# Second weight product of two MLPs with tokens on the output partitions, added to x straight from PSUM

## The reference, cut to what matters

```python
# layer 0
x_in = x
h = film(rmsnorm(x, norm2_w), cond, film2_w, film2_b)
h = gelu(h @ mlp_w1 + mlp_b1) @ mlp_w2 + mlp_b2        # 256 -> 1024 -> 256
x = x_in + h
# layer 1
h = rmsnorm(x, g2) * (1 + scale2) + shift2
a, gate = split(h @ w_fc + b_fc)                        # 256 -> 2048
x = x + (a * silu(gate)) @ w_fo + b_fo                  # 1024 -> 256
```

## Time and profile before

| | us |
|---|---|
| median of 3 runs | 2149.85 (2148.05 to 2149.91) |
| the profiled execution | 2150.09 |
| its span on the core | 2148.3 |
| TensorE busy | 2049.8 (95%) |
| VectorE busy | 1314.9 (61%) |
| ScalarE busy | 987.4 (46%) |
| GpSimd busy | 405.0 (19%) |
| mean granted TensorE clock | 0.993 of full |

### The profile page before, as it was taken

One profiled execution on the slowest core, in us unless ns is written; L12 is line 12 of the kernel. 1 busy time (PEld: TensorE's weight loads), 2 busy tenths in 40 slices (PEclk: granted clock), 3 DMA queues, 4 the chain that ended last, 5 costly groups with the idle time before them and its releaser, 6 DMA issues.

```text
span 2148.3 us, 44435 instructions
## 1 busy us (share of the span) xinstructions
PE 2049.8 (95%) x15652; PEld 1670.8 (78%) x15652; DVE 1314.9 (61%) x2537; ACT 987.4 (46%) x1581; POOL 405.0 (19%) x381
## 2 busy tenths in 40 slices
PE   7999999999999999999999999998999999998998
PEld 6887887778777888877777777776888777787887
DVE  5856565767766565654444555456666677775664
ACT  3444555444444333334444444445444555454443
POOL 3632112223221010101111111112001222210000
PEclk9999999999999999999999999999999999999999
DMA  6000000000000000000000000000000000000000
GB/s 224 21 10 8 7 11 15 9 7 15 7 8 13 18 20 10 20 5 7 7 6 5 5 0 5 5 2 16 5 5 5 16 6 10 10 1 9 21 20 30
DMA packets 18405, 33.38 MB, mean 16 GB/s; under 512 B 1298, under 2 KB 12050, under 8 KB 17810
## 3 DMA queue, kind: packets, MB, share of 16 engines
q1 hardware_dynamic: 18322, 32.25, 4.7%
HBM read 28.06 MB, written 4.19 MB: 15 GB/s over the span
## 4 chain that ended last, share of the span: by engine, by line
PE 79%; DVE 9%; issue 7%; ACT 2%; POOL 2%; DMA 0%; DVEq 0%; SPq 0%; ACTq 0%; POOLq 0%
PE psum L591 21%; PE psum L593 20%; PE psum L592 19%; PE psum L688 4%; PE psum L701 3%; PE psum L633 2%; PE psum L720 2%; PE psum L786 2%; PE psum L734 2%; PE psum L677 1%; DVE xn L1093 1%; PE psum L526 1%; DVE h_lo L1114 1%; DVE pb L1169 1%; PE psum L685 1%
## 5 line engine op out<-in xcount | busy, mean ns | idle before, releaser
L591 PE MATMUL psum<-h_hi,w_lo 128*128 128x512 f32 x1120 | 463.4, 414 | 11.7 <-DVE h_lo L1114 6.3
L593 PE MATMUL psum<-h_hi,w_hi 128*128 128x512 f32 x1120 | 441.6, 394 | 0.0
L592 PE MATMUL psum<-h_lo,w_hi 128*128 128x512 f32 x1120 | 440.8, 394 | 0.0
L1221 DVE TENSOR_TENSOR hid_lo<-hid,hid_hi 128x512 fp32r<-128x512 f32 x256 | 194.0, 759 | 266.2 <-ACT hid_hi L967 265.9
L967 ACT ACTIVATE hid_hi<-hid 128x512 fp32r<-128x512 f32 x256 | 161.7, 632 | 223.1 <-PE psum L593 133.0
L591 PEld LDWEIGHTS psum<-h_hi,w_lo 128*128 128x128 f32 x1120 | 212.4, 190 | 62.4 <-issue 11.0
L593 PEld LDWEIGHTS psum<-h_hi,w_hi 128*128 128x128 f32 x1120 | 211.8, 189 | 49.5
L592 PEld LDWEIGHTS psum<-h_lo,w_hi 128*128 128x128 f32 x1120 | 212.6, 190 | 39.0
L1303 POOL TENSOR_TENSOR rstd<-ms,half_t 128x4 f32<-128x4 f32 x64 | 65.4, 1021 | 903.9 <-DVE ms L1088 485.1
L1166 DVE TENSOR_REDUCE mx<-psum 128x8 f32<-128x512 f32 x192 | 132.4, 690 | 160.0 <-PE psum L677 106.7
L962 ACT ACTIVATE hid<-psum,vec 128x512 f32<-128x512 f32 x192 | 131.8, 687 | 182.8 <-PE psum L593 166.9
(11 more groups left out here) (140 smaller groups left out, 3601.1 us busy)
## 6 DMA issues: line engine op xcount, KB each, us to landing
stage<-in_w_dram SPq DMA_DIRECT2D x24, 256.0 KB, 2.7
stage<-in_w_dram SPq DMA_DIRECT2D x8, 512.0 KB, 3.5
out_dram<-xres SPq DMA_DIRECT2D x8, 512.0 KB, 2.9
xres<-in_x_dram SPq DMA_DIRECT2D x1, 3584.0 KB, 18.4
modw_mod<-in_modw_dram SPq DMA_DIRECT2D x2, 1536.0 KB, 13.6
stage<-in_w_dram SPq DMA_DIRECT2D x8, 384.0 KB, 3.3
stage<-in_w_dram SPq DMA_DIRECT2D x8, 192.0 KB, 2.4
modw_film<-in_modw_dram SPq DMA_DIRECT2D x1, 1024.0 KB, 7.4
```

The lines of the kernel that those rows point to most:

```text
L591: nc.tensor.matmul(dst, s_lo, m_hi, start=start and j == 0, stop=False)
L592: nc.tensor.matmul(dst, s_hi, m_lo, start=False, stop=False)
L593: ins = nc.tensor.matmul(dst, s_hi, m_hi, start=False, stop=stop and j == len(pairs) - 1)
L1221: nc.vector.tensor_tensor(hid_lo[:, slot, :], hid32[:, slot, :], hid_hi[:, slot, :].bitcast(F32), ALU.subtract).then_inc(sem["hid"], 1)
```

## The change

In the MLPs of layers 0 and 1 (layers 2 and 3 keep their form):

- `down` k takes the hidden piece as the stationary operand, 128 tokens at a time, and the weight (256 columns) as the moving one: 4 tiles by 3 instructions of 256 columns in place of 2 by 3 of 512. The result has tokens on the partitions, in the layout that `xres` has.
- ScalarE's two `y` instructions and the eight transposes of `back` are gone. VectorE's `back` adds `wide` to `xres` directly.
- `down` 0 of a block waits for `x_done` of the block before, since VectorE's add now reads `wide`.
- The bias is a row that is the same on all partitions. A new VectorE stage, `bias`, adds it to the block's `xres` (128 by 1024 elements) beforehand. The two rows are made once at the start: two copies on VectorE, four products with the identity, two copies out of PSUM.
- The order is changed: `back` of the block before comes first, and `bias` stands between `down` 0 and `stats`.
- A buffer of 1024 bytes (`down_bias1`) is placed ahead, and the padding before `at_hi` is changed, so that this buffer and those behind it (`hid32`, `hid_hi`, `hid_lo`, and all weights `w_hi`, `w_lo`) start at 64 bytes further, counted modulo 256. `h_hi`, `h_lo`, `xn` stay where they were.

```diff
     if kind == "mlp":
-        return [own("up", 2), own("down", 0), nxt("stats"), prev("back"), own("share"), own("up", 3), nxt("norm"),
+        back = [prev("back"), own("up", 2), own("down", 0), own("bias"), nxt("stats")] if layer < 2 else \
+            [own("up", 2), own("down", 0), nxt("stats"), prev("back")]
+        return back + [own("share"), own("up", 3), nxt("norm"),
...
-        at[0] += 32 - at[0] % 64
+        at[0] += (160 - at[0]) % 256
         at_hi = place("at_hi", [P, 2, BLK], F32R)
...
+                for m in range(2 * DC):
+                    ins = nc.tensor.matmul(psum[:, T_BANK + 1, m * P:(m + 1) * P], down_col[:, m, :], ident,
+                                           start=True, stop=True)
                 ins.then_inc(vo_product, 1)
...
                     pe.wait_ge(sem["hid"], n_at("hid", ph, b, k + 1))
-                    if k == 0:
+                    if k == 0 and layer < 2:
+                        pe.wait_ge(sem["x_done"], n_at("x_done", ph, b, 1))
+                    elif k == 0:
                         pe.wait_ge(sem["out_rows"], n_at("out_rows", ph, b, 0))
-                    for m in range(DC):
+                    for t in range(TILES if layer < 2 else 0):
+                        tok = slice(t * P, (t + 1) * P)
+                        ins = project(wide[:, t // 2, (t % 2) * D:(t % 2 + 1) * D],
+                                      [((hid_hi[:, slot, tok], hid_lo[:, slot, tok]), weight(ph, "down", k, 0, D))],
+                                      start=k == 0 and t % 2 == 0, stop=k == HID - 1 and t % 2 == 1)
+                    for m in range(DC if layer >= 2 else 0):
...
-                elif s == "down" and k == HID - 1 and layer in (0, 1):
-                    act.wait_ge(sem["down"], n_at("down", ph, b, HID))
-                    act.wait_ge(sem["back"], n_at("back", ph, b, 0))
-                    for m in range(DC):
-                        nc.scalar.activation(y[:, m, :], wide[:, m, :], ACT.Identity,
-                                             bias=col(f"d{layer}", m)).then_inc(sem["out_rows"], 1)
...
+                for n in range(2):
+                    nc.vector.tensor_copy(down_bias[n][:, :], psum[:, T_BANK + 1, n * D:(n + 1) * D]).then_inc(vo_cols, 1)
...
+                elif s == "bias" and kind == "mlp":
+                    xs = xres[:, bass.ds(b * TILES, TILES), :]
+                    nc.vector.tensor_tensor(xs, xs, down_bias[layer][:, :].unsqueeze(1).to_broadcast([P, TILES, D]),
+                                            ALU.add).then_inc(sem["biased"], 1)
+                elif s == "back" and kind == "mlp" and layer < 2:
+                    dve.wait_ge(sem["down"], n_at("down", ph, b, HID))
+                    dve.wait_ge(sem["biased"], n_at("biased", ph, b, 1))
+                    xs = xres[:, bass.ds(b * TILES, TILES), :].rearrange("p (w t) d -> p w (t d)", w=2)
+                    nc.vector.tensor_tensor(xs, xs, wide, ALU.add).then_inc(sem["x_done"], 1)
```

More of the change, by code:

```diff
@@ L158, in counts_of @@
                   "hid32": HID, "hid_hi": HID, "hid": HID, "down": HID, "gate_in": HID if layer == 1 else 0,
-                  "back": 1})
+                  "back": 0 if layer < 2 else 1, "out_rows": 0 if layer < 2 else 2, "biased": 1 if layer < 2 else 0})
         return c
@@ L254, in build @@
         half_t = place("half_t", [P, TILES], F32)
+        down_bias1 = place("down_bias1", [P, D], F32)
         no_seq = place("no_seq", [P, 2], F32)
@@ L265, in build @@
         rot_at = at[0]
+        down_bias = [place("down_bias0", [P, D], F32, rot_at), down_bias1]
         q2_sb = place("q2_sb", [P, 2, BLK], F32)
@@ L307, in build @@
         vo_col = place("vo_col", [P, 2 * DC, P], F32, wa + 16384)
+        down_col = place("down_col", [P, 2 * DC, P], F32, wa + 21504)
         vo_bias = place("vo_bias", [P, D], F32, wa + 18432)
@@ L566, in fold_vo @@
                 pe.wait_ge(wv_t_done, 1)
-                pe.wait_ge(vo_cols, 2)
+                pe.wait_ge(vo_cols, 4)
                 for m in range(DC):
@@ L777, in stage_of @@
                     ins.then_inc(sem["down"], 1)
-                elif s == "back" and ph:
+                elif s == "back" and ph and not (kind == "mlp" and layer < 2):
                     pe.wait_ge(sem["out_rows"], n_at("out_rows", ph, b, 2))
@@ L1000, in _ @@
             nc.vector.memset(pb[:, :, :], 0.0).then_inc(consts_ready, 1)
-            for n, name in enumerate(("v0", "o0")):
-                nc.vector.tensor_copy(vo_col[:, n * DC:(n + 1) * DC, :],
+            for n, name in enumerate(("v0", "o0", "d0", "d1")):
+                dst = (vo_col, down_col)[n // 2]
+                nc.vector.tensor_copy(dst[:, n % 2 * DC:(n % 2 + 1) * DC, :],
                                       col(name, 0, DC).unsqueeze(2).to_broadcast([P, DC, P])).then_inc(vo_cols, 1)
@@ L1325, in stage_of @@
                     mask_of_block(ph, k, b)
-                elif s == "bias":
+                elif s == "bias" and kind == "attn":
                     if is_first(b):
-                        pool.wait_ge(vo_cols, 3)
+                        pool.wait_ge(vo_cols, 7)
                     pool.wait_ge(sem["normed"], n_at("normed", ph, b, 1))
```

## The result

The changed kernel takes 2182.22 us (median, 2179.28 to 2184.92), the one before 2148.95 in the same series (2148.01 to 2149.91). The ratio is 1.0155, 95% interval 1.0137 to 1.0172: 33 us or 1.55% slower. The profiled execution took 2179.28 us, its span is 2177.4 (+29.1), its mean granted clock 0.988.

A forecast was written before the change was run, and what follows sets the result against it. TensorE was taken to bound the kernel, with three quarters and more of the chain. Terms 11.1 + 5.7 + 10.5 + 2.2 - 0.9 - 2.4 + 0.4 = 26.6 us on 2150.1, less 0.2, gave 2176.5 us; range 2154 to 2190.

The forecast's parts named there:

- The forecast case: Whole kernel: new waits outweigh the removed transposes, 2176.5 us, likeliest case spanning 2166 to 2187; chance 0.58.
- The wait before `down` 0: Block boundaries: VectorE's add queues behind `hid_lo` of piece 1, delaying `down` 0 by 2.26 us in layer 0, 0.95 in layer 1.
- The clock: Layer 0 boundaries: idle TensorE drops to 1.2 GHz, costing 1.4 us at 4 of 7, +5.7 us, ends 0 and +10.
- Rival B: Same waits, but second ones cost nothing or the clock stays up: 2160 to 2166 us, 2157 with cheap products; chance 0.21.
- The second wait: Bias add delays `xn`: 0.2 us per block in layer 0; 1.2 to 1.4 before second half of `up` 5, layer 1.
- The narrow products: `down`, layers 0 and 1: 12 products of 256 columns cost 1.39 us like 6 wide ones; ends -3.8 and +4.9 us.
- rival C: All 512-column products: the 64-byte move shortens them; break-even 5.1 ns each, full 18 ns gives 2083 us; chance 0.09.
- D: The move lengthens products, or all 7 waits bring the low clock and `down` costs 1.43: 2186 to 2191 us; chance 0.08.
- E: Block boundaries: the add gets ahead of `hid_lo`, so no wait appears and 2135 us results; chance 0.04.

The follow-up runs named there:

- addresses alone: Kernel before with only the padding line changed, moving hid, at and all weights 64 bytes further modulo 256: 2137.44 us, ratio 0.9962.
- token form with early add and late bias: Changed kernel with VectorE's add to `xres` right behind `down` 7 and the bias add moved to behind `down` 5: 2139.07 us, ratio 0.9956.
- early add alone: Changed kernel with VectorE's add that frees `wide` placed right behind `down` 7, ahead of the `hid_lo` for which it waited: 2148.31 us, ratio 1.0007.
- filled wait: Changed kernel with nine unread 512-column products ahead of the wait for `x_done`, at six of layer 0's seven boundaries: 2174.46 us, ratio 1.0119.
- all operands at 96: Kernel before with `xn` and all buffers behind it, `h`, hidden pieces and weights among them, at 96 modulo 256 bytes: 2136.55 us, ratio 0.9946.
- old padding: Changed kernel with the old padding line, buffers back at their old addresses modulo 256: 2189.9 us, ratio 1.0206.
- bias late alone: Changed kernel with only the bias add moved, from between `down` 0 and `stats` to after `down` 5: 2168.63 us, ratio 1.0103.

## Why the prediction was right, and by what it was off

The forecast case came: 2182.2 against 2176.5, inside the range (2154 to 2190) and on the side that was given 0.84. A ladder of four kernels splits the 33.3 us: before, addresses alone (0.9962), token form with early add and late bias (0.9956), early add alone (1.0007), the whole change (1.0155). Each step of the ladder is uncertain by some 5 us.

| step of the ladder | forecast | measured |
|---|---|---|
| addresses | 0 | -8.2 |
| transposes and `y` gone, narrower products, start | -13.9 - 1.5 + 0.4 = -15.0 | -1.3 |
| bias add ahead of `stats` | +9.9 + 1.4 + 2.2 = +13.5 | +11.0 |
| add behind `hid_lo`, clock included | +15.8 + 5.7 + 6.7 = +28.2 | +31.8 |
| sum | 26.7 | 33.3 |

(The forecast's numbers are those of its terms, regrouped: 16 x 0.87, 1.5 of the last block, the start; 7 x 1.42 and 7 x 0.2 of second waits and 2.2 at the ends; 7 x 2.26, the clock, 7 x 0.95; the last digit of the sum is rounding. The measured ones are the differences of the ratios, of 2149 us.)

- **The wait before `down` 0** was right in kind, and in size in layer 0. Idle time 2.12 for "some 2.1"; 0.97 in layer 1 for 0.8. The same order in the earlier trace rows gave both numbers. The experiment with the early add shows that it is the place in VectorE's queue that costs, and not the add itself.
- **The clock** was sized too low by count: 4 of 7 boundaries were forecast, 6 of 7 came, at 1.2 us each by the filled wait, for 1.4 forecast. 7.2 us against 5.7. Rival B's cheaper half (the clock stays up) was wrong.
- **The second wait** was right in layer 1 (1.15 before `up` 5, for 1.2 to 1.4), and its chain as well: bias add 1.22, `rstd`, `w_lo`, `xn` at its side. Only the order of arrival was other than told: `xn` came 0.29 us behind `w_lo`, not ahead of it, and so ended 0.94 after it, for 1.0. In layer 0 TensorE waited 0.10 us at the turn in the block without low clock, for 0.2, and not at all in the others. That block is 26.13, 2.22 over the one before, for 1.59; one of layer 1 is 2.10 over, for 1.5. Of the 0.6 above in each, 8 x 0.045 = 0.36 are the narrow products; the rest is not accounted for.
- **The narrow products** are the term that was mis-sized, and with the addresses they are most of the error. "I take the middle, 1.39: no cost" stands against 12 x 0.1194 = 1.43 us, the upper end that the forecast gave: +0.045 per `down`, some 6 us over 128. Of the two durations of the earlier trace rows the longer one held, that of `at`, with either address. And since the wide products got shorter elsewhere, to 0.2272, the narrow form gives up that gain too, and so do the `up` products beside it (231 ns in layer 0 and 230 in layer 1, 227.6 and 227.9 with the addresses alone). Why these stay long isn't settled. So the transposes' 13.9 us were nearly all spent. Set against the addresses alone, as in the ladder, an estimate from the distances is 16 x 0.55 = 8.8 for the narrow products, 2.1 for `up`, and 7 x 0.35 = 2.4 for the wait that stays in layer 1: 13.3 of the 13.7 missing.
- **The addresses** were rival C, and its mechanism was real, at 3.5 of the 18 ns: 8 to 12 us (the ratios 0.9962 and 0.9946, and 1.0155 against 1.0206), not the 26.6 that it needed to decide. The forecast named 1 ns as the point from which it would be wrong; by that test this step was wrong. What failed is the sentence against it: "the products of `h` and of the moved `hid` (as moving operands) have the same 0.231 now, so no gain by the address is seen at this width". The weights are moved as well and take part in both products, so equal times of the two showed nothing about the address. The 6 ns between `at` and `h` at 256 columns, named for it, were indeed of the address, but with the other sign: the move made the `h` products as long as those of `at`.
- **D and E**: some products did become longer through the move, as in D, clearly so the 480 of 256 columns with `h` stationary, but that is 1.7 us; no 512-column product of the MLPs did. The add does not get ahead of `hid_lo`.

The two errors, 8.2 us of gain missed and 13.7 of a gain that wasn't there, cancel in part; the total came within 6 us of the forecast for this reason too, and that much of it was luck.

The best of the kernels run here are the one before with all operands at 96 (0.9946), the early add with the late bias (0.9956) and the one before with the addresses of the change (0.9962). Their intervals overlap.

## What to carry to other kernels

When a stage takes over the job of freeing a buffer, look up what stands ahead of it in its engine's queue, and find a place in the old trace with that order: here it gave the way from that instruction to the first product to 0.01 us. Of such an instruction the place can be worth more than the form: here 32 us against 1, each within some 5. Price an instruction that is halved by the distance of its starts in both widths, and compare it with the wide one as it will be after the change, not as it is.

## What the runs showed of the hardware

- The start addresses of the buffers matter by themselves. In MLPs whose products are all of 512 columns, these start 227 to 228 ns apart with the split `h`, the hidden pieces and the weights all at the same address modulo 256 bytes (160 or 96), and 229 to 233 with the four placements in which they differ. In attention, and beside the 256-column products of the new form, 512-column products with `h` moving lie 229 to 231 ns apart though all agree. 256-column products with `h` stationary are shorter where it differs from the weights (114.7 to 115.8 ns before) than where it agrees (119 to 120).
- An idle time of TensorE of 2.1 us in a stretch of full work was followed by the lower clock (1.2 in place of 2.4 GHz) in 6 of 7 cases, in which 17 instructions got through in 4.1 us in place of 28; each cost 1.2 us. It was 6 of 7 as well in the runs with the old padding and with the bias late alone. Products that nobody reads, put into the idle time, kept the clock up.
- Four `xn` instructions took 3.28 us beside GpSimd's `w_lo` and 1.13 free of it; the first, begun 0.29 us into `w_lo`, lasted until 0.16 after its end. The Trainium skill ("SBUF — State Buffer", SBUF: two separate sides) describes a port pair shared by the two engines; the trace agrees.
